# A three-layer audio block in fp32 on one core: the norm before the first feed-forward moves to ScalarE, the clears of k's levels to GpSimd, in a new written-out order of all engines

## The reference

```
h = dct(frames)
a = layernorm(h)                       # outer norm, then the block's own norm: both are folded into two factors
# attention with decay, 4 heads of 32 channels
xq, xk, xv, xg = a * tm + shifted(a) * (1 - tm)
q, k = exp(rmsnorm(xq Wq)), exp(rmsnorm(xk Wk)); v = xv Wv; g = sigmoid(xg Wg)
A_t = lam * A_(t-1) + k_t v_t;  z_t = lam * z_(t-1) + k_t
x = a + (g * (q_t A_t) / (q_t z_t)) Wo
x = x + gelu(layernorm(x) W1) W2       # first feed-forward
h1 = h + x
# expert layer: norm, attn_w, then expert b % 8
y = layernorm(h1); xa = norm(y) Wat + y
out = h1 + gelu(gelu(xa fc1) fc2 Wnext)
```

## Time and profile before

| | us |
|---|---|
| median of 3 runs | 1095.11 |
| lowest, highest | 1094.64, 1097.32 |
| the profiled execution: time | 1096.16 |
| the profiled execution: span of the trace | 1094.2 |

### The profile page before, as it was taken

How to read it: one execution, slowest core, us unless ns; L and a number is a source line. 1 busy time by engine, 2 the same in 40 slices (tenths; PEclk the granted TensorE clock), 3 DMA queues, 4 the chain that set the end, 5 groups by cost and what they waited for, 6 DMA issues and landing times.

```text
span 1094.2 us, 44745 instructions
## 1 busy us (share of the span) xinstructions
PE 1058.0 (97%) x18851; PEld 796.5 (73%) x18851; DVE 919.4 (84%) x2848; ACT 648.0 (59%) x1128; POOL 304.8 (28%) x174
## 2 busy tenths in 40 slices
PE   6679999999999999999999999999999999999997
PEld 6557787786777777777777877777677777777763
DVE  5998988889888888988889898988888888899642
ACT  4346666656765566666566666655576656666533
POOL 4032233242132423313242232324213332331220
PEclk9799999999999999999999999999999999999999
DMA  6232332123323123332212333221332321223210
GB/s 219 88 109 70 97 99 67 53 78 98 98 73 115 54 58 93 97 98 70 83 56 87 98 97 98 71 75 53 97 98 80 102 69 54 89 80 98 80 30 18
DMA packets 51510, 91.55 MB, mean 84 GB/s; under 512 B 9552, under 2 KB 26608, under 8 KB 51312
## 3 DMA queue, kind: packets, MB, share of 16 engines
q1 hardware_dynamic: 51312, 88.69, 26.7%
HBM read 19.50 MB, written 9.78 MB: 27 GB/s over the span
## 4 chain that ended last, share of the span: by engine, by line
PE 93%; DVE 4%; issue 1%; ACT 1%; DMA 1%; SPq 0%; DVEq 0%
PE bank L987 13%; PE bank L1136 11%; PE bank L992 11%; PE bank L1158 10%; PE bank L1129 10%; PE bank L1164 10%; PE bank L1091 7%; PE bank L1066 4%; PE bank L1069 3%; PE bank L1109 3%; PE bank L1074 2%; PE bank L1152 2%; PE bank L1029 2%; PE bank L1113 2%; PE bank L1018 2%
## 5 line engine op out<-in xcount | busy, mean ns | idle before, releaser
L424 POOL TENSOR_TENSOR t_sum<-x,hs 128x512 f32<-128x512 f32 x32 | 40.8, 1276 | 529.9 <-DVE x L795 529.9
L1136 PE MATMUL bank<-w,hid 128*128 128x128 f32 x1024 | 122.7, 278 | 1.5 <-ACT hid L554 1.5
L1158 PE MATMUL bank<-xa,f1w 128*128 128x512 f32 (+1 forms) x256 | 121.1, 570 | 1.9 <-issue 1.8
L574 ACT ACTIVATE hid<-bank,f1b 128x512 f32<-128x512 f32 (+1 forms) x128 | 81.2, 647 | 69.6 <-PE bank L1158 67.7
L1136 PEld LDWEIGHTS bank<-w,hid 128*128 128x128 f32 x1024 | 116.7, 192 | 4.1 <-DVE x L795 1.6
L1129 PE MATMUL bank<-c,w 128*128 128x512 f32 (+1 forms) x256 | 115.8, 565 | 0.9 <-ACT c L548 0.9
L428 POOL TENSOR_TENSOR rr<-vv,nhalf 128x8 f32<-128x8 f32 x32 | 72.3, 2260 | 133.5 <-DVE vv L675 133.5
L1164 PE MATMUL bank<-hid,f2w 128*128 128x512 f32 (+1 forms) x256 | 107.6, 563 | 0.7 <-ACT hid L574 0.7
L1091 PE MATMUL bank<-qx,ki 128*32 128x16 f32 x7680 | 101.0, 193 | 5.7 <-DVE ki L847 5.7
L1091 PEld LDWEIGHTS bank<-qx,ki 128*32 128x32 f32 x7680 | 92.7, 110 | 17.4 <-issue 13.3
L554 ACT ACTIVATE hid<-bank 128x512 f32<-128x512 f32 (+1 forms) x128 | 70.3, 562 | 51.4 <-PE bank L1129 50.4
(11 more groups left out here) (139 smaller groups left out, 2402.9 us busy)
## 6 DMA issues: line engine op xcount, KB each, us to landing
qx<-qq SPq DMA_DIRECT2D x256, 96.0 KB, 2.4
hs<-hs SPq DMA_DIRECT2D x32, 532.0 KB, 3.4
v<-v_f SPq DMA_DIRECT2D x16, 512.0 KB, 3.3
gz<-gate_f SPq DMA_DIRECT2D x16, 512.0 KB, 4.0
xT<-in_xT SPq DMA_DIRECT2D x16, 468.5 KB, 3.5
f1w<-in_fc1T SPq DMA_DIRECT2D x16, 256.0 KB, 3.6
f2w<-g_dram SPq DMA_DIRECT2D x16, 256.0 KB, 3.7
out<-t_sum SPq DMA_DIRECT2D x16, 256.0 KB, 2.4
```

What stands on the lines that cost most here:

```text
L1136: last = mm(dst[:, P * i:P * i + P], hid[:, j, P * m:P * m + P], w2[:, j, :], start=(j == 0), stop=(j == 3))
L1158: mm(dst[:, 0:width[g]], f1w[:, P * j:P * j + P], xa[:, cols(g)], start=True, stop=True).then_inc(f1_ok, 1)
```

## The change

Three things are changed together.

- `normed2` goes from VectorE to ScalarE. VectorE computes only the offset -mean * r of four tiles (`offset2`, a new tile `nb2` and a new semaphore), and ScalarE computes r * x + offset for each tile.
- The clears of `ko` and `kw` go to GpSimd's start, that of `ki` to GpSimd behind `pow1` of sample 0. VectorE still waits for their semaphores.
- The lists of all five engines and the table of PSUM banks are written anew. A sample's stages now stand at other places of a round. `oTs` has `at(2)` instead of `at(3)` on TensorE, the second half of k's product `at(1)`, and on VectorE, GpSimd and SyncE most functions count one round more.

The cut diff:

```diff
@@ USES
-    [("qT0", 1), ("w1_01", 2), ("kT1", 1), ("w1_13", 2), ("nmT0", 2), ("f1_02", 2), ("nT1", 0), ("f1_10", 2), ("f1_13", 2), ("f2_1", 2)],
-    [("w1_00", 2), ("dct1", 0), ("w1_03", 2), ("g0", 1), ("w1_10", 2), ("zt", 1), ("f1_01", 2), ("n1T1", 2), ("oT0", 2), ("q0", 0), ("n2T0", 1)],
-    [("kT0", 1), ("v0", 1), ("w1_02", 2), ("g1", 1), ("rT0", 1), ("f1_03", 2), ("nT0", 0), ("at1", 2), ("f1_12", 2), ("k0", 0)],
...
+    [("n2T0", 2), ("w1_00", 2), ("w1_02", 2), ("v0", 1), ("g0", 1), ("w1_10", 2), ("dct1", 0), ("nmT0", 2), ("at0", 2), ("n1T1", 2), ("nT0", 0), ("f1_13", 2), ("oT1", 2)],
+    [("kT0", 1), ("v1", 1), ("w1_13", 2), ("qT1", 1), ("zt", 1), ("rT1", 1), ("nT1", 0), ("wo0", 1), ("f2_1", 2), ("k0", 0)],
+    [("wo1", 2), ("qT0", 1), ("w1_11", 2), ("f1_01", 2), ("f1_03", 2), ("f2_0", 2), ("f1_12", 2), ("q1", 0)],
+    [("w1_01", 2), ("w1_03", 2), ("w2_0", 2), ("dct0", 0), ("kT1", 1), ("u", 1), ("n1T0", 2), ("f1_00", 2), ("nmT1", 2), ("at1", 2), ("f1_10", 2), ("q0", 0)],
+    [("k1", 1), ("n2T1", 2), ("g1", 1), ("w1_12", 2), ("w2_1", 2), ("rT0", 1), ("f1_02", 2), ("f1_11", 2), ("oT0", 2)],
@@ gpsimd
+            gp.memset(ko[:, :, :], 0.0)
+            gp.memset(kw[:, :, :], 0.0).then_inc(s_lvo, 1)
             gp.wait_ge(s_init, 2)
...
                 gp.tensor_tensor(rr1[:, :, :], vv1[:, :, :], ..., ALU.pow).then_inc(r1_ok, 1)
+                if first(b):
+                    gp.memset(ki[:, :, :], 0.0).then_inc(s_lev, 1)
@@ scalar
+            def normed2(b, g):
+                act.wait_ge(nb2_ok, nth(b, 2, g + 1))
+                before(act, n1T_ok, b, 2, g + 1)
+                for m in tiles(g):
+                    last = nc.scalar.activation(nl2[:, m, :], x2[:, m, :], ACT.Identity, scale=rr2[:, m:m + 1], bias=nb2[:, m:m + 1])
+                last.then_inc(nl2_ok, 1)
@@ vector
-            def normed2(b, g):
+            def offset2(b, g):
                 dve.wait_ge(r2_ok, nth(b, 2, g + 1))
-                before(dve, n1T_ok, b, 2, g + 1)
-                for m in tiles(g):
-                    last = V.tensor_scalar(nl2[:, m, :], x2[:, m, :], mv2[:, m, 0:1], rr2[:, m:m + 1], ALU.subtract, ALU.mult)
-                last.then_inc(nl2_ok, 1)
+                V.scalar_tensor_tensor(nb2[:, four(g)], mv2[:, four(g), 0], -1.0, rr2[:, four(g)], ALU.mult, ALU.mult).then_inc(nb2_ok, 1)
...
-                    V.memset(ki[:, :, :], 0.0).then_inc(s_lev, 1)
...
-                    V.memset(ko[:, :, :], 0.0)
-                    V.memset(kw[:, :, :], 0.0).then_inc(s_lvo, 1)
```

More of the change, by code:

```diff
@@ L616, in body @@
                     attn_in(b)
+                if (b := at(0)) is not None:
+                    hlT(b, 0); hlT(b, 1)
                 if (b := at(2)) is not None:
@@ L866, in body @@
                 if (b := at(1)) is not None:
-                    zmul(b)
+                    normed(b)
+                if (b := at(2)) is not None:
+                    merge(b, 3)
+                if (b := at(3)) is not None:
+                    x_attn(b, 1)
+                if (b := at(2)) is not None:
+                    between(b, 1); inside(b, 1); gated(b, 0)
+                if (b := at(1)) is not None:
+                    shifted(b)
+                if (b := at(2)) is not None:
+                    merge(b, 4)
@@ new lines, in body @@
+                if (b := at(1)) is not None:
+                    mixes(b, 0)
+                if (b := at(2)) is not None:
+                    attended(b, 0); stats2(b, 0); merge(b, 5)
+                if (b := at(1)) is not None:
+                    mixes(b, 1)
+                if (b := at(2)) is not None:
+                    offset2(b, 0)
+                if (b := at(1)) is not None:
+                    sums(b, 0, 0)
+                if (b := at(3)) is not None:
+                    result(b, 0)
@@ new lines, in body @@
+                if (b := at(1)) is not None:
+                    sums(b, 0, 1); mixes(b, 2)
+                if (b := at(3)) is not None:
+                    result(b, 1)
+                if (b := at(2)) is not None:
+                    merge(b, 6)
+                if (b := at(1)) is not None:
+                    sums(b, 1, 0); sums(b, 1, 1)
+                if (b := at(2)) is not None:
+                    merge(b, 7)
+                if (b := at(1)) is not None:
+                    norms(b, 0); tokens(b, 0, 0)
@@ new lines, in body @@
+                if (b := at(2)) is not None:
+                    gated(b, 1)
+                if (b := at(1)) is not None:
+                    tokens(b, 0, 1); mixes(b, 3); norms(b, 1)
+                if (b := at(2)) is not None:
+                    attended(b, 1); stats2(b, 1)
+                if (b := at(1)) is not None:
+                    tokens(b, 1, 0)
+                if (b := at(2)) is not None:
+                    offset2(b, 1)
+                if (b := at(1)) is not None:
+                    tokens(b, 1, 1); qlev(b, 0)
@@ L868, in body @@
+                if (b := at(2)) is not None:
+                    hidden(b, 0); stats3(b, 0)
+                if (b := at(1)) is not None:
+                    between(b, 0); inside(b, 0); decayed(b)
                 if (b := at(2)) is not None:
                     normed3(b, 0)
+                if (b := at(1)) is not None:
+                    zscan(b); from_start(b); zmul(b); chain(b)
+                if (b := at(2)) is not None:
+                    hidden(b, 1)
+                if (b := at(1)) is not None:
+                    merge(b, 0)
@@ L872, in body @@
                 if (b := at(1)) is not None:
[L873 removed]
+                    denominators(b)
+                if (b := at(2)) is not None:
+                    stats3(b, 1); x_attn(b, 0)
                 if (b := at(0)) is not None:
                     stats1(b, 1)
[L876 to L877 removed]
+                if (b := at(1)) is not None:
+                    merge(b, 1)
                 if (b := at(0)) is not None:
                     variance1(b)
[L880 to L881 removed]
                 if (b := at(1)) is not None:
[L883 to L887 removed]
+                    gate(b, 0)
                 if (b := at(2)) is not None:
@@ L890, in body @@
                 if (b := at(1)) is not None:
-                    merge(b, 2); gate(b, 0); gate(b, 1)
-                if (b := at(0)) is not None:
-                    normed(b)
-                if (b := at(1)) is not None:
-                    merge(b, 3); between(b, 1); inside(b, 1)
-                if (b := at(2)) is not None:
-                    x_attn(b, 1)
-                if (b := at(0)) is not None:
-                    shifted(b)
-                if (b := at(1)) is not None:
-                    gated(b, 0)
@@ L926, in body @@
-                if (b := at(2)) is not None:
-                    result(b, 1)
-                if (b := at(0)) is not None:
-                    qlev(b, 0)
-                if (b := at(1)) is not None:
-                    merge(b, 7)
-                if (b := at(0)) is not None:
-                    between(b, 0)
-                if (b := at(1)) is not None:
-                    gated(b, 1)
-                if (b := at(0)) is not None:
-                    inside(b, 0)
-                if (b := at(1)) is not None:
-                    attended(b, 1); stats2(b, 1)
@@ L940, in body @@
-                if (b := at(0)) is not None:
-                    mixes(b, 3); from_start(b)
-                if (b := at(1)) is not None:
-                    normed2(b, 1); hidden(b, 0)
-                if (b := at(0)) is not None:
-                    merge(b, 0); decayed(b); zscan(b)
-                if (b := at(1)) is not None:
-                    stats3(b, 0)
+                    merge(b, 2); gate(b, 1); qlev(b, 1)
             every_round(body)
```

229 lines of the change are left out of this document (94 added, 135 removed), and 2 rows, old and new, of the table USES.

## The result

The changed kernel takes 1091.69 us, the median of 10 runs (1089.64 to 1093.9), beside 1095.6 (1094.64 to 1097.32) of the kernel before on the same chips: a ratio of 0.9962, interval 0.9952 to 0.9972. It is faster by 3.9 us (0.4%). 14.9 were forecast, and 1091.69 lies above the range given, by 0.7 us.

What follows compares the result with a forecast made beforehand. TensorE's stream was taken to bound the steady rounds, VectorE the fill, the last sample's chain the drain: 88.7 + 13 x 64.5 + 152.1 = 1079.3 us of span, plus 0.9, 1080.2 us; range 1073 to 1091.

Steps and rivals of the forecast that it cites:

- The period: Steady rounds, set by TensorE's own stream: DCT to DCT of successive samples, 64.5 us forecast, between 64.37 and 64.9.
- `f1s` stall: TensorE's `f1s(0,2)` and `f1s(0,3)` took 2.08 us instead of 1.72, waiting for VectorE's `gate`; 0.36 us a round should go.
- rival C: Slower: ScalarE reaches `normed2(1)` late behind its queue and TensorE waits; period 66.07, time 1100.6 us; chance 0.10.
- the short value: GpSimd's power before the second norm takes 1.02 us, not 1.90, so the norm comes on time, not 0.4 us late.
- the 0.13 allowed: Allowance in us a round for the norm's new wait and the other close places, on top of 64.37.
- 13 x 64.5: The middle of the span, from sample 2's DCT to sample 15's, as 13 periods of 64.5 us each.
- 13 x (64.82 - 64.5): Gain forecast in the middle: 4.2 us, from the old average period of 64.82 to the new 64.5.
- So GpSimd's part is hidden.: Clears on GpSimd take 2.2 and 3.5 us, in place at about 10 and 18, before products needing them at 34.
- The fill: Start to sample 2's DCT, set by VectorE: DCT at 88.7 us, 10 us won in like terms, bounds 6.0 and 12.
- Rival B: Loads, tanh or half clock hold TensorE in the fill; only the 4.0 us wait goes: +6, 1086.2 us; chance 0.13.
- The drain: From the last DCT to the end: 152.1 us against 165.5; 12.8 of the 13.4 less is the DCT's new place.
- From span to time: Step from the forecast span of 1079.3 us to the median time of 1080.2, adding 0.9 us as before.

## Why the prediction was wrong

*The period.* Right in mechanism: the `f1s` stall went, the norm is on time, rival C's queue did not form. The power took 1006 to 1017 ns in all 32 places, the short value. That agrees with the prediction's reading of the Trainium skill (SBUF — State Buffer, "SBUF: two separate sides"). The size was off: 64.65 for 64.5, 2.0 us over 13 rounds, of which 0.06 a round is the norm on ScalarE and 0.22 two small waits (against the 0.13 allowed) whose cause stays open.

*"13 x 64.5".* This step failed. It took all 13 periods as steady ones. The earlier trace rows already gave 64.82 on average against 64.73: 1.17 us in one round, which the prediction noticed and never explained. It counted the difference as something that the change would gain back ("13 x (64.82 - 64.5)"). Instead late blocks and what followed took 3.3 us of the new middle; in the other profiles of the new order it was 0.1 to 4.1, the run with clears beside everything left out.

*"So GpSimd's part is hidden."* This is the other step that failed. The clears were asked only when they are in place, not what runs beside them: 3.0 us on VectorE at the head of the fill, where all work waits. The prediction asked of the power what runs beside it on VectorE, where that spoke for the change, and did not ask it of the clear.

*The fill.* With the DCT's new place taken off (12.8 us, as the prediction did), 5.5 us were won where 10 were forecast. The timetable itself was close: with the clears out of the way sample 2's DCT stood at 89.9 and 90.1, for 88.7 forecast. Of the 4.6 us missing in the first profile about 3 are the exclusion (3.2 in the medians); the cause of the rest, 1.2 to 1.4, stays open. Rival B was partly right: in the kernel before, taking 6.5 us off VectorE and putting 3.0 on the norm gave 1 to 2 us, not 3.5.

*The drain.* As forecast: 152.96 for 152.1.

*From span to time.* 0.9 us was added; the profiled run has 1.98, so the median of the runs is 1.7 above its span. Together 4.6 in the fill, 5.3 in the middle, 0.9 in the drain and 0.8 here are, but for rounding, the 11.5 us between 1080.2 and 1091.69.

## What to carry to other kernels

Before work goes to an idle GpSimd, look at what VectorE does in just those microseconds: a `tensor_scalar` or a copy from SBUF to SBUF ended here only when the clear beside it did. A wait of one line puts the clear beside sums and mixes of two sources, which it did not lengthen. In a kernel whose TensorE is full, compare the mean of the periods with their median first: what lies between them belongs to single rounds and no reordering can be credited with it. A gain under 4 us of 1090 needs several profiles before it is put down to a place, for one execution differs from the next by that much. And before two runs are called the same experiment, compare their instruction counts.

## What the runs showed of the hardware that was not expected

- TensorE's instructions arrive 256 at a time, 16 KB in 0.9 to 2.4 us each in the profile after. In a middle of 843 us none to five blocks came late, at 0.3 to 1.4 us each, always at the same record of the 256 and nearly always at the same dense stretch of the round.
- Half clock came in the middle as one stretch of 3.4 us, each time 3 to 5 us behind such a gap; the transposes of four tiles in it at 754.8 took 1.01 us instead of 0.60 to 0.66.
- A clear of 640 columns took 628 to 725 ns, of 4096 columns 3.5 us; one VectorE instruction of 340 ns took 3.1 us longer beside it.
